# Grouping the routing of two expert layers as four, three and one batches instead of four, two and two

## The reference, cut to what matters

```python
# first mixture (L0_ffn): top 2 of 8
logits = einsum('bsd,ed->bse', x, w_router)
top_vals, top_idx = top_k(logits, 2)
router_weights = softmax(top_vals)
...
# second mixture (L1_ffn): softmax over 8, top 2; of the chosen two the one
# with the higher number sets the row, so one expert per row is worked out
logits = einsum('bsd,de->bse', x, gate_w) + gate_b
scores = softmax(logits); topk_s, topk_i = top_k(scores, 2)
...
    h = relu(xf * wi @ w1[i] + b1[i]); y = h @ w2[i] + b2[i]
    out = where(wi > 0, y, out)
```

## Time and profile before

| | |
|---|---|
| profiled execution | 1745.63 us, of which 1743.8 us is the span of the trace |
| median of three runs | 1737.9 us |
| PE busy | 1557.0 us, 89% of the span |
| DVE busy | 910.1 us, 52% |
| ACT busy | 678.8 us, 39% |
| POOL busy | 412.5 us, 24% |
| first drain and first mixture's routing | about 320 to 366 us of the span |
| second drain and second mixture's routing | about 820 to 862 us of the span |

### The profile page before, as it was taken

One profiled execution on the slowest core, in us unless ns is written; L12 is line 12 of the kernel. 1 busy time (PEld: TensorE's weight loads), 2 busy tenths in 40 slices (PEclk: granted clock), 3 DMA queues, 4 the chain that ended last, 5 costly groups with the idle time before them and its releaser, 6 DMA issues.

```text
span 1743.8 us, 40008 instructions
## 1 busy us (share of the span) xinstructions
PE 1557.0 (89%) x14902; PEld 1287.8 (74%) x14902; DVE 910.1 (52%) x2316; ACT 678.8 (39%) x1611; POOL 412.5 (24%) x627
## 2 busy tenths in 40 slices
PE   7998998789995889998699599997998999999998
PEld 6876776678994667776588477775786776789897
DVE  3665777521105557778311364567344555566764
ACT  3334776322333236654122323662663444211110
POOL 2224776510004331111100134552111111000101
PEclk9998999999997999999899799998999999999999
DMA  5443000188971002110578201101002100033232
GB/s 206 150 155 136 29 27 17 52 294 290 323 250 49 2 1 83 30 29 12 214 281 297 88 1 46 42 27 49 2 1 69 35 29 2 25 121 98 91 105 68
DMA packets 41852, 166.76 MB, mean 96 GB/s; under 512 B 5984, under 2 KB 16864, under 8 KB 30176
## 3 DMA queue, kind: packets, MB, share of 16 engines
q1 hardware_dynamic: 39392, 159.14, 26.3%
q0 software_dynamic: 2304, 5.51, 1.0%
HBM read 140.22 MB, written 24.41 MB: 94 GB/s over the span
## 4 chain that ended last, share of the span: by engine, by line
PE 69%; DVE 13%; issue 8%; DMA 3%; POOL 3%; ACT 2%; SPq 1%; DVEq 0%; POOLq 0%; ACTq 0%
PE bank L1996 6%; PE bank L2009 6%; PE bank L1389 4%; PE bank L1938 4%; PE bank L1940 4%; PE bank L1939 4%; PE bank L1376 3%; PE bank L857 2%; PE bank L866 2%; DMA xrow<-slots 2%; PE bank L831 2%; PE bank L958 2%; PE bank L1403 1%; PE bank L1364 1%; PE bank L1359 1%
## 5 line engine op out<-in xcount | busy, mean ns | idle before, releaser
L3664 POOL TENSOR_TENSOR mv<-mv,cst 112x1 f32<-112x1 f32 x88 | 20.7, 235 | 583.1 <-DVE mv L2684 583.1
L2603 ACT ACTIVATE htile<-bank,wup 128x128 f32<-128x128 f32 x280 | 79.9, 369 | 190.1 <-PE bank L1996 190.1
L2378 ACT ACTIVATE arena<-big,nm 112x375 f32<-112x375 f32 x256 | 143.7, 605 | 23.4 <-DVE nm L3348 14.4
L1389 PEld LDWEIGHTS bank<-cst,arena 112*125 112x125 f32 x768 | 100.8, 197 | 44.6 <-issue 22.0
L1996 PE MATMUL bank<-xtile,wup 128*128 128x128 f32 x1120 | 133.0, 278 | 0.3 <-DVE xtile L3511 0.2
L1996 PEld LDWEIGHTS bank<-xtile,wup 128*128 128x128 f32 x1120 | 130.0, 194 | 1.0 <-DVE xtile L3511 0.9
L3527 DVE COPY yrow<-bank 128x256 f32<-128x256 f32 x35 | 14.9, 425 | 217.6 <-PE bank L2009 217.6
L2009 PE MATMUL bank<-wdn,htile 128*128 128x256 f32 x560 | 126.3, 379 | 0.0
L1389 PE MATMUL bank<-cst,arena 112*125 112x112 f32 x768 | 116.0, 290 | 8.4 <-POOL arena L3838 4.7
L2009 PEld LDWEIGHTS bank<-wdn,htile 128*128 128x128 f32 x560 | 103.9, 190 | 12.7
L3838 POOL TENSOR_SCALAR arena<-arena,c_lo 112x375 f32<-112x375 f32 x64 | 98.2, 1547 | 37.1 <-ACT c_lo L2382 37.0
(11 more groups left out here) (386 smaller groups left out, 3728.4 us busy)
## 6 DMA issues: line engine op xcount, KB each, us to landing
wup<-in_moe_up SPq DMA_DIRECT2D x35, 1028.0 KB, 7.3
wdn<-in_moe_dn SPq DMA_DIRECT2D x35, 1024.0 KB, 6.0
vspace<-in_ring SPq DMA_DIRECT2D x40, 512.0 KB, 3.9
ctxs<-parts SPq DMA_DIRECT2D x30, 564.0 KB, 3.9
slots<-mlpw SPq DMA_DIRECT2D x11, 1024.0 KB, 6.4
parts<-ctxs SPq DMA_DIRECT2D x8, 564.0 KB, 3.1
xrow<-slots SPq DMA_DIRECT2D x35, 128.0 KB, 5.1
slots<-yrow SPq DMA_DIRECT2D x35, 128.0 KB, 7.0
```

What stands on the lines that cost most here:

```text
L1389: mm = pe.transpose(bank[4 + (3 * g + t) % 2][0:KT, j * T:(j + 1) * T], c_pr[:, g, j, t * KT:(t + 1) * KT], ident[0:T, 0:T])
L2378: nc.scalar.activation(c_pr[:, g, j, :], c_sc[:, g % 2, j, :], ACT.Exp, bias=nm[:, p, h:h + 1], scale=-1.0).then_inc(cexp_done, 1)
L2603: ins = nc.scalar.activation(htile[:, g % 2, m, :], bank[2 + 2 * (g % 2) + m // 4][:, m % 4 * ROWS:(m % 4 + 1) * ROWS], func, bias=wup[:, ...
```

## The change

The middle group takes three batches and the last one. Since the third batch of the middle group, batch 6, has its `xT` only in the drain, the whole work on the middle group moves there: in both mixtures its logits from `s` 7 to `s` 11 on TensorE, its reading and maxima from the start of step (8, 0) ("7.5") to the end of step 11 on VectorE; in the second mixture its masks and weights from 8 and 12 to 12, its ranks from 13 to 14, and its exponentials on ScalarE from (8, 0) to (8, 3).

```diff
-CHUNKS = ((0, 4), (4, 6), (6, 8))
+CHUNKS = ((0, 4), (4, 7), (7, 8))
...
                     s = 4 * (b - B + 2) + g
-                    ranked_at = (3, 13) if nr == 0 else (5, 13)
-                    if s not in (0, 7) + ranked_at:
+                    ranked_at = (3, 13) if nr == 0 else (5, 14)
+                    if s not in (0, 11) + ranked_at:
                         return
                     pe.wait_ge(cmax_ready, at(sub, "c16", min(b, B - 1), 4 * (g if b < B else 3) + 1))
-                    if s in (0, 7):
-                        route_logits(nr, s // 7, "L1_router" if nr else "L0_router")
+                    if s in (0, 11):
+                        route_logits(nr, s // 11, "L1_router" if nr else "L0_router")
...
-                    if sub.index == 4 and isinstance(b, int) and (b, g) in ((B - 2, 3), (B, 0)):
+                    if sub.index == 4 and isinstance(b, int) and (b, g) in ((B - 2, 3), (B, 3)):
                         route_exps(1, 0 if b < B else 1)
...
-                    elif s == 7.5:
+                    elif s == 11:
                         route_read(0, 1)
                         route_top(0, 1)
...
-                    elif s == 7.5:
+                    elif s == 11:
                         route_read(1, 1)
                         route_top(1, 1)
                         route_below(1, slice(*CHUNKS[1]))
-                    elif s == 8:
+                    elif s == 12:
                         route_hot(1, 1)
                         dve.wait_ge(rt_exp, 3)
-                        route_weights(1, slice(*CHUNKS[1]), 0)
-                    elif s == 12:
-                        route_weights(1, slice(*CHUNKS[1]), 1)
+                        route_weights(1, slice(*CHUNKS[1]))
...
-                        route_scaled(SUBS[5], 4, 6)
+                        route_scaled(SUBS[5], *CHUNKS[1])
...
-                    if sub.index in (1, 4) and isinstance(b, int) and (b, g) == (B, 0):
-                        route(sub, 7.5)
```

## The result

The changed kernel takes 1747.49 us (median of 20 runs, 1737.58 to 1755.06), the kernel before, run beside it, 1741.76 (median of 20, 1735.17 to 1751.57). The ratio is 1.0036 with a 95% interval of 1.0020 to 1.0052, on 1741.76 us 3.5 to 9.1 us slower. The prediction was +7.7 us, a ratio of 1.0044, and slower at 0.72. Its time of 1745.6 us rests on the three runs known then; the longer series puts the kernel before 3.9 us higher than those three did, and the change itself at some 2 us less than forecast, so the times agree better than the two parts do. The profiled execution after took 1750.31 us.

The account below looks back on a forecast made before the run. In both drains one chain going to and fro between engines, mainly TensorE and VectorE, was taken to set the time, not any engine's amount of work. 3.0 + 4.7 = +7.7 us gave 1745.6 us, range 1739 to 1751.

Parts of the forecast that it names:

- The held copy: VectorE's L2716 stands behind the middle group's reading and maxima: 3.4 us later in the first drain, 3.8 in the second.
- Ahead of the drains: Routing leaves step (8, 0): 0 in the first mixture, a gain of 0.9 us in the second, between 0 and 1.06.
- The second drain: Second mixture, batch 7's output to the table: the table 4.7 us late, bounds 3.5 and 5.6.
- wait for the ranks: Second drain: VectorE's middle-group slots wait for L838, the ranks and hand-over, 1.4 us.
- last group saves: Shorter work for the last group as one batch: 1.1 us in the first drain, 1.0 in the second.
- The first drain: First mixture, batch 7's output to the expert-row load: 3.0 us late, bounds 2.4 (only table) and 3.6 (only sends).
- the fall of the clock: Rival, chance 0.18: TensorE's idle time in the first drain brings 1.2 GHz, costing 2.8 us more, 1748.4 us.
- The sends: First drain, POOL's eight sends: landing at 362.55 against 362.2 by the table's path, too near to tell which holds.
- The sum: Both drains together: 3.0 + 4.7 = +7.7 us, 1745.6 us against the median of the three runs.
- rule of the Trainium skill: Grouping can help a saturated engine; smaller pieces may be sooner where VectorE is unsaturated but awaited; prediction took the second half.
- Hidden: Rival, chance 0.10: the work fits VectorE's idle time in the drains and L2716 is not held; -3.0 us, 1734.9.
- Absorbed: Rival, chance 0.12: slack in the first mixture's table and sends, short ranks' wait in the second; +1.5 and +2.8, 1742.2 us.

Follow-up runs that it names:

- first records: The first profiled executions of the kernel before and the changed kernel; these executions took 1745.63 and 1750.31 us.
- Both versions with the block in the holes: Kernel before, second mixture's middle-group routing moved into VectorE's idle times: 1737.49 us, ratio 0.9991; the same with eight filler products before the ranks: 1739.40 us, 1.0005.
- seven records of this order: Changed kernel twice, first mixture alone twice, late place with groups 4, 2, 2, ranks ahead of L838, three sends fewer; times from 1740.80 to 1752.86 us.
- the record with the fillers: Changed kernel with eight more filler products on TensorE (ten in place of two) ahead of L857; 1748.38 us in one execution.
- the second record: Each kernel executed once more, unchanged: the changed kernel took 1752.86 us, the kernel before 1745.14 us, one execution each.

## Why the prediction was right

**The held copy: right, in both drains.** The block of reading and maxima stands in front of L2716. Forecast 3.4 and 3.8, measured 3.00 and 3.62. The excess is the gap of 0.35 that I added behind the routing from rows 8: it is not there in the first drain and 0.24 in the second. The logits took 1.28 against 1.36.

**Ahead of the drains: right.** In the first, nothing was forecast: batch 7's L850 stands 19.46 us behind batch 6's for 19.39 in the first records and 18.50 for 18.49 in the second. In the second 0.9 was forecast and 0.95 measured, and the wait of 1.06 before the last products is gone. Both versions with the block in the holes show the same 0.9.

**The second drain: right, each term a little large.** Against before and less the gain, L2723 is 4.2 late (forecast 4.5), the reading 5.3 (5.7), the table 4.25 (4.7). The wait for the ranks was put at 1.4 and is 1.34; taking it away brings 0.9 back, since some 0.4 of hand-over stays. The last group saves 1.03 (1.0).

**The first drain: the size by two errors that cancel in part.** I named the fall of the clock as a rival with 0.18 and left it out of the forecast. It is in all seven records of this order. The granted clock is 0.50 from 344 to 346, L857 costs 0.93 more (0.9 worked out), and the fillers run over; the whole is 1.2 to 2.2 us, not 2.8. My argument against it, that TensorE works on both sides of the wait and has a clock of 0.89 over the stretch, was an average over 46 us set against a wait of 1.9. The second drain's own row, 2.00 us of idle time and then 0.50, was the nearer one. At the full clock, in the record with the fillers, the table is 2.66 late for 2.4 forecast, and the load 2.54 for 3.0. Some 0.27 of this at the table lie in two instructions of that record, L3243 (0.37 us for 0.16) and L3256 (0.23 for 0.16). In the profiled record after, the last group saves 0.63 between its reading and the table, 0.67 worked out. With the clock the table is 3.6 late and the load 3.8, for 3.0 forecast.

**The sends: half right.** The table alone and the sends alone were thought equally near. In the profiled record the sends hold the load, by 0.6 us, of which some 0.4 was there before; in the second record the table alone does. What the sends cost at the first expert product is open.

**The sum.** To the loads: 3.8 and 5.02 - 0.95 = 4.1 us, 7.9 for 7.7 forecast; between the second records it is 4.7 and 4.0, 8.7. To the first expert products, for which 3 and 4.7 more were named, it is 3.4 and 3.8 between the first records and 6.2 and 4.2 between the second. That 7.7 lies so near is in part luck, since the held copy was put 0.4 too high and the clock at nothing. The timing says 3.5 to 9.1, with 5.7 between the medians. Of the 2 us between the forecast and the medians part may be given back in the first expert stage. From the first to the last block of L1996 it takes 148.6 us on average in the nine records whose first drain is that of the change, and 149.7 in the five where it is that of before, but the records of one code alone spread over 2.5 us (147.90 and 150.41 after). That is open, as is what part of the first drain's loss reaches the end.

**The rivals.** "Hidden" needed L2716 not to be held; it is. "Absorbed" needed a short wait for the ranks; it is 1.34. Of the rule of the Trainium skill, "Perfetto Trace Analysis", section "Optimizing Scalar/DVE Operations", neither half shows here. The first asks for a saturated engine, and VectorE is busy for 52%. For the second, narrower instructions in the same place are as slow: those between L2716 and L2723 take 3.14 us with three batches and 3.09 with two in the second drain. There they cost their number, not their width, and what decides is whether they stand in the chain.

## What to carry to other kernels

When work is moved on an engine that runs in written order, ask first whether the next critical instruction stands behind it, and then whether the block fits between the two ends of that chain at all; putting it behind the first hand-over helps little if it is longer than the hole. Where the move leaves TensorE idle in a serial tail for as long as another place of the same trace where its clock fell, give the fall more than 0.18 and put its price into the sum by that chance: here it came in seven of seven records, behind an idle time of 1.88 us elsewhere in one of two. For a change of some 5 us in 1740, segments between two named instructions tell the mechanism to a tenth of a microsecond, while even ten or twelve executions of each kernel tell only the sign, or not that.

## What was not expected of the hardware

The same instructions with the same idle time (1.91 and 1.90 us) gave a clock that fell ahead of L857 in one execution and behind it in the other, 1.0 us apart at the load. Eight filler products of 128x256, 1.72 us more of TensorE's time (2.40 for 0.68), kept the clock. From the issue of `xrow` to the first products that need it the time moved from 6.2 to 8.0 us between records whose routing and loads are the same or nearly so (6.26 and 8.02 with one kernel), more than most of the terms that were forecast.
